# Layer 2's projections, window branch and latent branch in one 48-step pipeline

## What is computed

```python
Q, K, V = heads(x @ wq), heads(x @ wk), heads(x @ wv)            # 16 heads of 8
sc  = einsum('bhnid,bhnjd->bhnij', Qb, Kw) / sqrt(D)              # windows of 32 queries, 64 keys
sc  = where(mask, sc, -inf)
local = einsum('bhnij,bhnjd->bhnid', softmax(sc), Vw)
GQ  = heads(x @ wgq); GK = pool(x @ wgk); GV = pool(x @ wgv)      # 8 heads of 8, 64 latents
lsc = where(lmask, einsum('bhsd,bhnd->bhsn', GQ, GK) / sqrt(LAT_HD), -inf)
rem = einsum('bhsn,bhnd->bhsd', softmax(lsc), GV)
...
out = (sigmoid(Q . gate_local) * local + sigmoid(Q . gate_remote) * (rem @ r_out_w)) @ w_out
```

## Time and profile before

| | |
|---|---|
| runs shown | 2080.85, 2083.96, 2085.77 us (median 2083.96) |
| the profiled execution | 2079.02 us, its span on the core 2077.2 us |
| busy in the span | PE 1726.9 us (83%), DVE 1427.1 (69%), ACT 1198.3 (58%), POOL 1135.7 (55%) |
| mean granted TensorE clock | 0.934 |
| the stretch that the change touches | from 697.59 to 923.58 us of the span |

### The profile page before, as it was taken

How to read it: one execution, slowest core, us unless ns; L and a number is a source line. 1 busy time by engine, 2 the same in 40 slices (tenths; PEclk the granted TensorE clock), 3 DMA queues, 4 the chain that set the end, 5 groups by cost and what they waited for, 6 DMA issues and landing times. The chain is left out here.

```text
span 2077.2 us, 30893 instructions
## 1 busy us (share of the span) xinstructions
PE 1726.9 (83%) x10655; PEld 1119.7 (54%) x10655; DVE 1427.1 (69%) x2106; ACT 1198.3 (58%) x2024; POOL 1135.7 (55%) x1025
## 2 busy tenths in 40 slices
PE   4637999999577588686878999899999999998988
PEld 1414777788543276452453555555555555555564
DVE  3374777773255588675228888888888888888883
ACT  3274333336246366334437877777778777777860
POOL 1053454542300276211323788888888788888881
PEclk9577999998589899897899999999999999999999
DMA  1212222220100000001412999989999999999993
GB/s 29 63 39 69 67 83 81 79 80 27 29 6 14 12 1 1 1 1 35 119 47 50 158 165 162 156 154 159 158 163 161 159 158 163 164 166 153 162 163 63
DMA packets 630967, 193.09 MB, mean 93 GB/s; under 512 B 591553, under 2 KB 622034, under 8 KB 630814
## 3 DMA queue, kind: packets, MB, share of 16 engines
q1 hardware_dynamic: 622342, 167.55, 44.9%
q0 software_dynamic: 8224, 23.51, 3.7%
q10 hardware_dynamic: 248, 0.06, 0.0%
HBM read 36.90 MB, written 12.48 MB: 24 GB/s over the span
## 5 line engine op out<-in xcount | busy, mean ns | idle before, releaser
L2917 DVE TENSOR_REDUCE half_max<-scores 128x1 f32<-128x1024 f32 x512 | 614.5, 1218 | 133.8 <-PE scores L2699 127.6
L2616 POOL TENSOR_TENSOR p_low<-p,p_high 128x2048 f16<-128x2048 f32 (+15 forms) x256 | 576.2, 2251 | 150.5 <-ACT p_high L2843 129.7
L2699 PE MATMUL scores<-k_high,q_pair 128*128 128x512 f16 x1024 | 304.4, 378 | 66.0 <-ACT p L2828 62.8
L2828 ACT ACTIVATE p<-scores,exp_bias 128x1024 f32<-128x1024 f32 (+7 forms) x384 | 317.4, 861 | 71.7 <-DVE exp_bias L2922 69.4
L2699 PE MATMUL scores<-k_low,q_pair 128*128 128x512 f16 x1024 | 304.8, 379 | 0.0
L2843 ACT ACTIVATE p_high<-p 128x2048 f16<-128x2048 f32 (+15 forms) x256 | 282.6, 1104 | 36.6 <-DMA pT_high<-p_high 26.8
L2719 PEld LDWEIGHTS scores<-v_pair,pT_high 128*128 128x128 f16 x2176 | 150.4, 98 | 102.0 <-issue 62.7
L2719 PE MATMUL scores<-v_pair,pT_low 128*128 128x129 f16 x2176 | 184.2, 220 | 12.1 <-DMA pT_low<-p_low 11.9
L2719 PE MATMUL scores<-v_pair,pT_high 128*128 128x129 f16 x2176 | 186.6, 220 | 3.2 <-DMA pT_high<-p_high 3.2
L2719 PEld LDWEIGHTS scores<-v_pair,pT_low 128*128 128x128 f16 x2176 | 145.5, 98 | 47.4 <-DMA pT_low<-p_low 16.6
L2699 PEld LDWEIGHTS scores<-k_low,q_pair 128*128 128x128 f16 x1024 | 99.3, 97 | 122.1 <-issue 0.8
(11 more groups left out here) (490 smaller groups left out, 3228.3 us busy)
## 6 DMA issues: line engine op xcount, KB each, us to landing
pT_high<-p_high SPq DMA_TRANSPOSE x256, 3.6
pT_low<-p_low SPq DMA_TRANSPOSE x256, 3.6
slots<-zero_row SPq DMA_DIRECT2D x1, 3036.0 KB, 14.4
slot_rows<-slots SPq DMA_DIRECT2D x23, 132.0 KB, 2.4
slots_out<-expert_out SPq DMA_DIRECT2D x23, 128.0 KB, 1.8
w_up<-in_L_ffn_inter_w_dram SPq DMA_DIRECT2D x1, 2048.0 KB, 10.6
dispatched<-moe_rows SPq DMA_DIRECT2D x1, 1024.0 KB
slot_rows<-dispatched SPq DMA_DIRECT2D x4, 256.0 KB, 3.9
```

The costliest lines, as they stand in the source:

```text
L2616: pool.tensor_tensor(flat(pl[:, buf, b0:b0 + n, :]), flat(p32[:, buf, b0:b0 + n, :]), flat(ph[:, buf, b0:b0 + n, :]), ALU.subtract).then_i ...
L2699: mm = pe.matmul(ps[:, b.start + i, :], q, k[:, par, cs(2 * half + i)], start=start, stop=not start)
L2828: act.activation(flat(p32[:, buf, b0 + first:b0 + first + w, :]), flat(ps[:, banks(p, half), :])[:, 0:w * P], ACT.Exp, bias=bias[:, p:p + ...
L2917: dve.tensor_reduce(mx[:, p % 2, half:half + 1], flat(ps[:, b[half], :]), AX.X, ALU.max, negate=True)\
```

## The change

Stages 1 to 3 become one, `l2_branches`, with one pipeline of 48 steps: 32 window steps, then 16 latent ones, in the same four softmax tiles and the same eight PSUM banks. The parts:

- **PE's order in a step.** Transposes of step s, front of step s+2, for the latent steps the query product of the step after that, then the output products of step s. DVE's order in a step stays.
- **Projections.** All eight products come first, in other PSUM banks; q and k are taken by ACT and DVE, two chunks of each per engine, and k goes straight from PSUM into its four head groups (sixteen passes of 512 columns, eight on each of ACT and DVE, in place of four copies and four passes of 2048).
- **Input windows.** POOL takes them from the input itself; the padded copy is gone (only the first window's 32 columns are cleared).
- **Latent constants.** DVE pools the tokens at the start, among the key cuts; the two projections follow in the same place on PE; DVE builds the key and value blocks between its second shift and the first sum, on tiles that POOL has cleared; POOL builds the latent mask in steps 4 to 8.
- **Outputs.** ACT copies out the latent outputs too, one instruction a step, in place of DVE. The gate weights are scaled by DVE after steps 0 and 1.

Two barriers go. The core of the diff:

```diff
-def l2_window(nc, m, inp, r):
+def l2_branches(nc, m, r, w, gate_w):
...
+    ALL = STEPS + NT
+    KCHUNKS = ((0, 2), (1, 3))
+    ORDER = (("k", 0), ("k", 1), ("q", 0), ("k", 2), ("k", 3), ("q", 1), ("q", 2), ("q", 3))
...
             @block.tensor
             def _(pe):
-                pe.wait_ge(k_cut, 4)
-                pe.wait_ge(padded, 3)
+                for unit in ORDER:
+                    kind, c = unit
+                    pe.matmul(proj[unit], w[:, 0 if kind == "q" else 1, :], m.xn[:, cs(c)], start=True, stop=True)\
+                      .then_inc(q_raw if kind == "q" else k_raw, 1)
+                pe.wait_ge(k_cut_act, 4)
+                pe.wait_ge(pooled, 3)
...
-                def body(s, k):
-                    if not isinstance(s, int) or s + 2 < STEPS:
-                        front(s + 2, k % 2)
-                    back(s, k)
-
-                front(0, 0)
-                front(1, 1)
-                steps(pe, body)
+                front(0)
+                front(1)
+                for s in range(ALL):
+                    turn(s)
+                    if s + 2 < ALL:
+                        front(s + 2)
+                    if STEPS <= s + 3 < ALL:
+                        latent_query(s + 3 - STEPS)
+                    weigh(s)
...
+                cut(KCHUNKS[1][0])
+                copy_q(0)
+                cut(KCHUNKS[1][1])
+                copy_q(2)
...
+                for s in range(ALL):
+                    par = s % 2
+                    if s + 1 < ALL:
+                        exp(s + 1)
                     act.wait_ge(turned, s + 1)
-                    if not before(s, 2):
+                    if s >= 2:
                         act.wait_ge(out_raw, s - 1)
                     act.activation(pt[:, par].rearrange("p a n -> p (a n)"), tps[:, par, :], ACT.Copy).then_inc(pt_ready, 1)
-                    if not before(s, 1):
-                        pick(s - 1, 1 - par)
+                    if s:
+                        pick(s - 1)
+                    if s + 2 < STEPS:
+                        values(s + 2)
+                    if STEPS <= s + 3 < ALL:
+                        latent_query(s + 3 - STEPS)
+                pick(ALL - 1)
...
-                def body(s, k):
-                    middle(s, k)
-                    if not isinstance(s, int) or s + 2 < STEPS:
-                        front(s + 2, (k + 2) % 4)
...
+                for s in range(ALL):
+                    middle(s)
+                    if s + 2 < ALL:
+                        front(s + 2)
```

More of the change, by code:

```diff
@@ L1880, in l2_window @@
[L1880 to L1901, removed]
+        pm, pool2 = sb("pooled_mean", [P, NL]), sb("pooled", [P, 2, NL])
@@ new lines, in l2_branches, with at, tile @@
+        gk, gv = sb("latent_keys", [P, LH, NL]), sb("latent_values", [P, 4, P])
+        gq = sb("latent_q", [P, 2, P])
+        ps = own.enter_context(psum(nc, "branches", [P, 8, CH]))
+        vps, sps, tps, ops = (ps[:, 2 * i:2 * i + 2, :] for i in range(4))
+        proj = {unit: ps[:, (4, 5, 6, 7, 1, 3, 0, 2)[i], :] for i, unit in enumerate(ORDER)}
+        cps = proj["k", 1]
+        with stage(nc, "gates", "q_raw", "k_raw", "q_ready", "q_ready_act", "k_cut", "k_cut_act", "padded", "masks_set", "v_zeroed",
+                   "mask_set", "pooled", "kv_raw", "blocks_zeroed", "blocks", "q_masked", "x_copied", "v_raw", "lq_raw", "lq_ready",
+                   "scored", "v_masked", "shifted", "maxed", "less_max", "exped", "totaled", "inverted", "p_ready", "turned",
+                   "pt_ready", "out_raw", "out_ready") as (
+                block, gates, q_raw, k_raw, q_ready, q_ready_act, k_cut, k_cut_act, padded, masks_set, v_zeroed,
+                mask_set, pooled, kv_raw, blocks_zeroed, blocks, q_masked, x_copied, v_raw, lq_raw, lq_ready,
+                scored, v_masked, shifted, maxed, less_max, exped, totaled, inverted, p_ready, turned,
+                pt_ready, out_raw, out_ready):
+            raw_count = lambda unit: [u for u in ORDER if u[0] == unit[0]].index(unit) + 1
+            def at(t, s):
+                return t[:, s * KW:s * KW + KW]
+            def tile(t, n):
+                return t[:, n * P:(n + 1) * P]
@@ L1988, in back, with weigh @@
                     mm.then_inc(turned, 1)
+                def weigh(s):
+                    k, par = s % 4, s % 2
                     pe.wait_ge(pt_ready, s + 1)
[L1990 to L1994, removed]
@@ L2006, in _, with cut @@
+                    mm.then_inc(out_raw, 1)
+                front(0)
[7 more added lines that the diff above has]
+                    weigh(s)
             @block.scalar
             def _(act):
-                def exp(s, k):
+                def cut(c):
+                    act.wait_ge(k_raw, raw_count(("k", c)))
+                    for g in range(4):
+                        act.activation(kg[:, g, WIN + c * CH:WIN + (c + 1) * CH], proj["k", c], ACT.Copy, scale=m.hmod[:, g:g + 1])\
+                           .then_inc(k_cut_act, 1)
@@ L2058, in _, with front @@
+                cut(KCHUNKS[0][0])
+                dve.wait_ge(pooled, 1)
+                dve.tensor_scalar(pm[:], pm[:], 1.0 / CHUNK, None, ALU.mult).then_inc(pooled, 1)
+                dve.wait_ge(pooled, 2)
+                dve.tensor_copy(pool2[:], pm[:].unsqueeze(1).to_broadcast([P, 2, NL])).then_inc(pooled, 1)
+                cut(KCHUNKS[0][1])
+                copy_q(1)
+                copy_q(3)
                 dve.wait_ge(masks_set, 12)
-                def front(s, k):
-                    par = k % 2
-                    if not before(s, 4):
+                def front(s):
+                    k, par = s % 4, s % 2
+                    if s >= 4:
@@ L2247, in _ @@
+                front(0)
+                front(1)
                 dve.wait_ge(kv_raw, 1)
-                dve.memset(gk[LD:P], 0.0).then_inc(blocks, 1)
+                dve.wait_ge(blocks_zeroed, 2)
                 dve.tensor_tensor(gk[0:LD], cps[0:LD, 0:NL].unsqueeze(1).to_broadcast([LD, LH, NL]),
```

390 lines of the change are left out of this document (147 added, 243 removed).

## The result

| | before | changed |
|---|---|---|
| median of the runs | 2083.65 us (2080.85 to 2085.77) | 2174.45 us (2172.96 to 2176.83) |
| span of the profiled execution | 2077.2 us | 2171.2 us |
| mean granted TensorE clock | 0.934 | 0.913 |
| first q and k product to first gate product | 226.0 us | 319.3 us |

What follows compares the result with a forecast made beforehand. PE's order, with a 0.69 us wait for ACT's copy, was taken as the bound. Start -7.4, windows +66.6, seam -11.2, latent +23.3 and drain -0.9 gave +70.4 us: 2154 us (chance 0.64), range 2112 to 2184.

Steps and rivals of the forecast that it cites:

- The turn-taking of PE and DVE: In each step, DVE's shift and PE's transposes wait for each other; window period 5.2 us against 3.60 at full clock.
- Latent: Period of the 13 steady latent steps: 5.15 us at full clock against 4.06 before.
- The first rival: All steps of the merged loop stay at 2.4 GHz: +37 us, 2121 us; chance 0.20.
- the lower end of the range: 2112 us: full clock throughout, with DVE's products 0.1 us shorter each (0.69 instead of 0.80) and a few at the start.
- The clock: PE's pause of about 2.2 us a step sometimes halves the clock; mean periods 5.9 us (window) and 5.85 us (latent).
- the pause ahead of 860.76: In the kernel before, PE stood still 1.98 us; the granted clock was then 0.50 from 861.1 to 867.9.
- The rule of the Trainium skill: Idle gaps between matmul bursts shorter than its stated length keep the clock up; the pauses worked out are shorter.
- a third of the steps (0.35) at half rate: Share of window and latent steps at 1.2 GHz, each 1.95 us longer; windows +66.6 us, latent steps +23.3 us.
- Start and seam: Start to the third shift 23.5 us from 30.9 (-7.4); window-to-latent seam 16.5 us from 27.7 (-11.2).
- POOL's list: POOL's work before the first front: 12.45 us less the 2.85 us input copy, plus a small memset, about 10.8.
- The drain: End of the latent steps, up to the first gate product: 9.2 us from 10.1, -0.9.
- POOL's latent mask: Mask building in steps 4 to 8 adds about 1.2 us to POOL, hidden in longer steps: costed at nothing.

Runs made afterwards that it cites:

- run 3: The changed kernel with three idle products of 256 columns on PE at the end of each step, used by nobody; 2127.86 us.
- run 4: The changed kernel with one idle product of 256 columns on PE behind each step's output products; 2132.22 us.
- run 5: The changed kernel with one idle product a step, placed late: PE issues it once DVE has the inverse of the next step; 2125.18 us.
- run 1: The changed kernel with PE's old order in a step put back: front of step s+2, then transposes, then output products; 2052.78 us.
- run 6: The changed kernel with PE's front three steps ahead instead of two, still between transposes and output products; 2022.36 us.
- run 7: The kernel of run 6 with POOL's latent mask moved out of steps 4 to 8 into POOL's idle times; 2018.73 us.

## Why the prediction was right, and where it was off

- **The turn-taking of PE and DVE** was right in kind and size. At full clock the period was worked out as 5.2; it is 5.23 in the changed kernel's step at 724.77 and 5.21 to 5.29 in run 3, where the shift waits 2.13 us (forecast: about 2.1). Latent: 5.15 forecast, 5.26 measured. The first rival's sum, +37 for the loop at full clock, compares with +42.9 in run 3's stretch (268.9 - 226.0). The shorter products of DVE (0.69) that the lower end of the range allowed for did not come: they still take 0.80 (862.52).
- **The clock** was right in kind. The falls came as the pause ahead of 860.76 suggested, and the first rival, with all steps at full rate, did not happen: its 2121 us is near what run 3 shows (2127.86) once the pause is filled. The rule of the Trainium skill cited above (TensorE: Matmul & The Clock Gate, section "Why this matters for your kernels") would have kept the clock up here; the runs do not agree, since all 25 pauses of 2.22 to 2.37 us, shorter than its limit, were followed by scores at half rate.
- **The step that was off** is "I therefore take a third of the steps (0.35) at half rate", in the window steps. Their period is 6.67, not 5.9, that is 0.75 of the 1.95 us between the two rates in place of 0.35: 29 x 0.77 = 22 us, the whole miss of 20 and a little more. The 0.35 was a choice between none and all, not worked out from rows, and 0.75 lies above the 0.65 that the range was drawn for. The reason I gave, that PE has less idle time left at half rate, holds only while the output products run at half rate as well (770.23: next pause 1.58). From 781.54 on the clock was back before them, the pause stayed 2.35 us, and the steps locked; I had not thought of a rate that changes twice within one step. In the latent steps, with a pause of 2.13 us at full rate, the mean came out (5.79 against 5.85), in part by luck: 6 of the 13 periods were long, more than a third, but by 0.6 to 1.4 us and not by 1.95. They bring the share over all 42 periods to 0.62, with which the time lies inside the range.
- **Start and seam** were right within 2 us: -9.1 for -7.4 and -11.6 for -11.2. The first front came 9.8 us after the first product (709.58 - 699.81), a microsecond sooner than its 10.8. The forecast took POOL's list for the bound; the wait that ended last was for DVE's copy of q, while POOL had the masked queries of the first two steps ready by 707.98:

```profile
709.58 0.71 PE L2026 MATMUL branches<-w_v,x_window 128*128 128x128 f32 x4 [0.52 <-DVE l_q L2172]
```

- **The drain** was forecast 9.2 and took 13.0. I counted its steps at full rate; the granted clock in it was 0.63. In runs 4 and 5, at full rate, it takes 10.65 and 10.54, so that some 2.4 of the 3.8 us are the clock and the rest was missing in the count. It is 10.1 in runs 1, 6 and 7.
- **POOL's latent mask** was costed at nothing, under long steps, and in this kernel it is: the periods of those steps do not stand out. With the cover gone (run 6) five periods are 0.5 to 0.8 us longer.

## What to carry to other kernels

When work is moved into an engine's idle time, ask who waits for that work: a pause of 0.69 us was filled here by delaying something that another engine needed at once, and the two engines then took turns. Moving it with one more step of lead gave the fill without the turn-taking. And a pause of about 2 us or more that comes back in every step is to be costed with a fall of the TensorE clock in it, unless the rows of a like kernel show that the clock holds; pauses of 0.69 us, as in the kernel before, left it at 1.00.

## What was not expected of the hardware

- Within one step of 6.83 us the granted clock goes down and up again, and the pattern repeats for 20 steps. A kernel that does more on PE can therefore be faster: three idle products a step took 47 us off.
- DVE instructions on SBUF and POOL's subtractions and selects beside them lengthened each other here. In these rows it is the one that began second that grew. DVE's product of 128 x 512 takes 0.81 us in the steady steps of run 6, 1.51 where it began just behind POOL's subtraction, and 1.26 where it began under a select. It takes 0.69 where the subtraction began after it, and then the subtraction takes 1.40 in place of 1.04:

```profile
728.74 1.04 POOL L1987 TENSOR_TENSOR branch_scores<-branch_scores,branch_stats 128x512 f32<-128x512 f32 x1
728.83 1.51 DVE L2216 TENSOR_TENSOR branch_scores<-branch_scores,branch_stats 128x512 f32<-128x512 f32 x1
...
732.52 0.69 DVE L2216 TENSOR_TENSOR branch_scores<-branch_scores,branch_stats 128x512 f32<-128x512 f32 x1
732.71 1.40 POOL L1987 TENSOR_TENSOR branch_scores<-branch_scores,branch_stats 128x512 f32<-128x512 f32 x1
...
739.18 1.14 POOL L1975 TENSOR_SCALAR_AFFINE_SELECT latent_mask<-latent_mask 32x1024 f32<-32x1024 f32 x1 [0.20 <-POOL q_masked L1960]
739.59 1.26 DVE L2216 TENSOR_TENSOR branch_scores<-branch_scores,branch_stats 128x512 f32<-128x512 f32 x1
```

  In run 7 the scaling of the gate weights, 0.28 us elsewhere, takes 1.10 behind the start of a moved select, and the select ahead of that one, which began behind a product of DVE, 1.62 instead of 1.14. The two periods there grew by 0.33 us. The other part of the missing gain lies in the expected 5 us itself: run 6's periods from step 5 to step 11 exceed 2.99 us by only 3.6 in all.
